# Merging two evictions, moving scale steps on VectorE, and moving the end of an attention chain by a third of an iteration

## The reference, cut to what matters

```python
x:  4 batches x 2048 tokens x 256
xn = layernorm(x)
# attention without softmax: per batch a 256 x 256 matrix and a bias
Q = l2norm(xn @ Wq.T + bq); K = l2norm(xn @ Wk.T + bk); V = xn @ Wv.T + bv
tailor = 1 / (L + Q . (sum(K) + EPS))
s = xn + gamma * (sum(V) + Q^T (K V)) * tailor
# feed forward, every operand quantized and dequantized to FP4 in blocks of 16
gate, up = fp4(xn) @ fp4(w_gate).T, fp4(xn) @ fp4(w_up).T        # 256 -> 704
g = silu(fp4(silu(gate) * up) @ fp4(w_down).T)                   # 704 -> 256
out = x + s * g
```

## Time and profile before

| | |
|---|---|
| median of three runs | 593.37 us |
| the profiled execution | 593.2 us, of which 591.5 us are the span from first to last instruction |
| PE busy | 547.5 us (93%) |
| DVE busy | 554.6 us (94%) |
| ACT, POOL busy | 415.6 us (70%), 243.4 us (41%) |
| granted TensorE clock | 0.987 over the span |

### The profile page before, as it was taken

The page is one execution under the profiler, slowest core; times in us unless marked ns, Lnnn a source line. Parts: engine busy times, 40 slices in busy tenths (PEclk is TensorE's granted clock), DMA queues, the critical chain, the costliest instruction groups (busy, mean ns, idle before and its releaser), DMA issues. The chain is left out here.

```text
span 591.5 us, 15211 instructions
## 1 busy us (share of the span) xinstructions
PE 547.5 (93%) x4973; PEld 424.9 (72%) x4973; DVE 554.6 (94%) x1180; ACT 415.6 (70%) x902; POOL 243.4 (41%) x213
## 2 busy tenths in 40 slices
PE   0478999999999999999999989999999999999996
PEld 0356777778787777778787767778787777778875
DVE  6998999999999999999999997999999999987783
ACT  4979888877787787767676766777776777555431
POOL 6524433333434434434443343444343344422146
PEclk9969899999999999999999999999999999999999
DMA  8010000000011001111011111110111101103124
GB/s 253 18 37 19 19 20 19 19 20 19 19 37 37 19 2 57 55 55 55 33 44 36 54 58 56 55 36 27 49 54 55 56 37 38 37 33 129 37 95 174
DMA packets 17633, 29.15 MB, mean 49 GB/s; under 512 B 2704, under 2 KB 5136, under 8 KB 17552
## 3 DMA queue, kind: packets, MB, share of 16 engines
q1 hardware_dynamic: 17552, 28.13, 14.3%
HBM read 19.73 MB, written 8.39 MB: 48 GB/s over the span
## 5 line engine op out<-in xcount | busy, mean ns | idle before, releaser
L1495 PE MATMUL GU<-wgu,xqT 128*128 128x352 f16 x1536 | 253.7, 316 | 3.6 <-issue 2.3
L1495 PEld LDWEIGHTS GU<-wgu,xqT 128*128 128x128 f16 x1536 | 148.5, 99 | 78.2 <-issue 3.4
L564 POOL TENSOR_TENSOR ht<-h,hrr 128x1408 f32<-128x1408 f32 x32 | 82.9, 2589 | 80.2 <-DVE hrr L992 78.7
L659 ACT ACTIVATE sil<-GU,wkap 128x352 f32<-128x352 f32 x128 | 70.7, 552 | 55.7 <-PE GU L1495 54.8
L1505 PE MATMUL DS<-wdT,hqT 128*128 128x256 f16 x704 | 87.3, 272 | 0.6 <-ACT hqT L666 0.6
L523 POOL TENSOR_TENSOR xnat<-xs,xnat 128x510 f16<-128x510 f32 (+1 forms) x32 | 37.0, 1157 | 106.1 <-DVE hq L1026 89.7
L1026 DVE TENSOR_TENSOR hq<-hg,hs 128x704 f16<-128x704 f16 x128 | 79.1, 658 | 1.0
L978 DVE SCALAR_TENSOR_TENSOR h<-GU,wkap,sil 128x352 f32<-128x352 f32 x128 | 68.7, 537 | 11.6 <-ACT sil L659 8.0
L1505 PEld LDWEIGHTS DS<-wdT,hqT 128*128 128x128 f16 x704 | 66.8, 98 | 10.4 <-ACT hqT L666 0.9
L513 POOL TENSOR_TENSOR rs<-ve,half 128x2 f32<-128x2 f32 x32 | 23.8, 744 | 110.0 <-DVE ht L1015 106.1
L695 ACT ACTIVATE gring<-DS,hun 128x256 f32<-128x256 f32 (+1 forms) x64 | 29.8, 465 | 42.9 <-issue 29.1
(11 more groups left out here) (176 smaller groups left out, 954.9 us busy)
## 6 DMA issues: line engine op xcount, KB each, us to landing
xin<-in_L_attn_x SPq DMA_DIRECT2D x34, 256.0 KB, 2.8
xe<-in_L_attn_x SPq DMA_DIRECT2D x24, 256.0 KB, 2.8
out<-o SPq DMA_DIRECT2D x24, 256.0 KB, 2.0
algebra<-in_L_ffn_w_down SPq DMA_DIRECT2D x1, 704.0 KB, 7.3
gring<-in_L_ffn_w_up SPq DMA_DIRECT2D x1, 640.0 KB, 6.1
xs<-in_L_attn_x SPq DMA_DIRECT2D x2, 256.0 KB, 4.2
xt<-in_L_attn_x SPq DMA_DIRECT2D x2, 256.0 KB, 4.8
out<-xin SPq DMA_DIRECT2D x2, 256.0 KB, 2.0
```

Source lines behind the costliest of these rows:

```text
L564: g.tensor_tensor(paired(ht[:, 0:2 * I]), paired(h[:, q]), spread(hrr[:, q], 4 * CB), ALU.mult).then_inc(S["ht_d"], 1)
L659: a.activation(sil[:, c], GU[:, c, 0, 0:CH], ACT.Silu, scale=wkap[:, 0:1]).then_inc(S["sil_d"], 1)
L1495: last = t.matmul(GU[:, c, m, 0:CH], xqT[:, k, j, 2 * a_ + kc], wgu[:, b_, kc, 2 * m + c], start=(z == 0 and kc == 0), stop=(z == 2 and kc ...
```

## The change

Three things change. The two y pieces of j = 0 are made by one instruction (`e_row`), which stands where the second one stood and counts two, except at `FIRST`. On DVE `x_scales` 1, 3 and 2 and `parts` 2 now stand ahead of `x_round` 0 and 1, and the y piece (1,0) stands behind `h_round` 2. In the attention tables the steps "top" and "high_low" are asked and answered elsewhere: "top" moves from (4,1,2) to (5,0,0) on PE and (5,0,1) on DVE, "high_low" from (5,0,1) to (5,0,2) on PE and from (5,0,4) to (5,0,2) on DVE. No tile, buffer or transfer changes.

```diff
-                (2, 1, 2): "norms", (3, 0, 2): "raw", (3, 1, 2): "tailor", (4, 0, 2): "product", (4, 1, 2): "top",
-                (5, 0, 1): "high_low"}
+                (2, 1, 2): "norms", (3, 0, 2): "raw", (3, 1, 2): "tailor", (4, 0, 2): "product", (5, 0, 0): "top",
+                (5, 0, 2): "high_low"}
...
-                   (3, 0, 0): "norms", (4, 0, 0): "tailor", (4, 0, 3): "scale", (4, 1, 0): "product", (4, 1, 2): "top", (5, 0, 4): "high_low"}
+                   (3, 0, 0): "norms", (4, 0, 0): "tailor", (4, 0, 3): "scale", (4, 1, 0): "product", (5, 0, 1): "top", (5, 0, 2): "high_low"}
...
+            def e_row(p, k, j):
+                e, q, row = s_place(p, k, j)
+                halves = lambda ap: ap.rearrange("p (c n) -> p c n", c=2)
+                wait(dve, "s_d", 4 * e + 2 * row + 2)
+                wait(dve, "g_d", 2 * e + row + 1)
+                v.scalar_tensor_tensor(halves(y[:, q, row * D:(row + 1) * D]), GU[:, :, 1, CH:CH + P], unm[:, 0:1],
+                                       halves(ring(gring, e, GRING)[:, row]), ALU.mult, ALU.mult).then_inc(S["y_d"], 2)
...
-                if s_beside(p, 0, tail):
-                    e_half(p, k, 0, 0, last_halves(0, i))
                 if s_beside(p, 0, tail) and last_halves(0, i):
+                    e_half(p, k, 0, 0, True)
                     e_half(p, k, 0, 1, True)
...
                 if s_beside(p, 0, tail) and not last_halves(0, i):
-                    e_half(p, k, 0, 1)
+                    e_row(p, k, 0)
...
                 attention(0, 2)
-                if on["xb"]:
-                    x_round(p, k, 0)
-                    x_round(p, k, 1)
-                if on["mb"]:
-                    parts(p, k, 2)
                 if on["xa"]:
                     x_scales(p, k, 1)
                 if on["xb"]:
                     x_scales(p - 1, 1 - k, 3)
+                if on["xa"]:
+                    x_scales(p, k, 2)
+                if on["mb"]:
+                    parts(p, k, 2)
+                if on["xb"]:
+                    x_round(p, k, 0)
+                    x_round(p, k, 1)
                 attention(0, 3)
                 if on["mb"]:
                     h_round(p, k, 0)
-                if on["xa"]:
-                    x_scales(p, k, 2)
                 if on["m"]:
                     h_mul(p, k, 1, 0, i)
-                if s_beside(p, 1, tail):
-                    e_half(p, k, 1, 0)
                 if on["xb"]:
                     x_round(p, k, 2)
...
                 if on["mb"]:
                     h_round(p, k, 2)
+                if s_beside(p, 1, tail):
+                    e_half(p, k, 1, 0)
                 if on["m"]:
                     h_mul(p, k, 1, 1, i)
```

## The result

The changed kernel takes 596.16 us (median of 7 runs, 594.67 to 597.98); the kernel before, on the same chip, takes 593.01 (7 runs, 592.32 to 593.45). The ratio is 1.0057, with a 95% interval of 1.0046 to 1.0068: 3.2 us slower, with 596.0 forecast. The profiled execution took 596.73 us, of which 595.0 are the span; it is 3.5 above the one of before. PEclk was 0.991.

A forecast was written before the change was run, and what follows sets the result against it. DVE was taken to set the pace, with PE having under 5 us of slack per batch. Terms +1.5 (first eleven iterations), -0.25 (iteration 11), +0.8 (loop), +0.8 (end) total +2.85 on 593.2: 596.0 us, range 589 to 599.

The forecast's parts named there:

- Merge: One 128x256 y instruction on DVE instead of two y pieces saves 0.13 us in each of 19 iterations.
- Dependent neighbours: DVE scale steps that read the result just ahead (xss behind xam, xrr) cost 0.14 us more in 29 iterations.
- Rival D: DVE steps reading the result just ahead cost nothing extra, so 4.1 us go away: 591.9 us; chance 0.03.
- Port waits at xt: With scale steps standing beside POOL's o instead of xt, DVE saves 1.9 us per batch; new loss 1.35.
- Port waits at hq: With y (1,0) between, the second hq pair meets POOL's xnat 0.26 us later, saving 2.1 per loop batch.
- Stalls of the lead: gate_up waits for later y, so DVE stalls at i = -1 and 0, 1, 2, 4: 3.9 us per batch.
- high_low: Now behind PE's down product, this attention step comes later than DVE wants it: 0.3 us stall in i = 5.
- The loop's +0.4 per batch: Eight loop iterations: DVE's own work changes by -3.8 us, new stalls add +4.2, so +0.4, twice.
- Iteration 11: Change of -0.25 us in this iteration: +0.14 for scale steps, -0.13 for merged y, -0.26 at hq.
- The end: From iteration 28 PE's chain runs to the end; gate_up (0,0) of 30 comes at 523.3, not 522.14: +0.8 us.
- Rival C: gate_up (1,0) waits for h (0,1); 20 iterations each pay about 0.25 us, loop lumps in full: 601; chance 0.07.
- Rival B: Gains and losses cancel: DVE gives up port waits where it then waits for PE; 593.3 us; chance 0.15.

## Why the prediction was right, and where only its sum was

The mechanism was right in part. DVE does save work and gets waits for PE in its place, whose gate_up is told of its free bank too late; y (1,0) late on the kernel before, and early in the changed one, show it from both sides. But the forecast had the loss in the wrong place. By its terms the late y costs -4.2 - 0.3 + 7.8 + 0.8 = +4.1 and the scale order 29 x 0.14 - 3.8 = +0.3. Each alone measured +1.2 and +3.1. That 596.0 stands beside 596.2 is luck in good part: terms missed in opposite ways.

- *Merge, -0.13 in 19 iterations.* Mis-sized: alone it gives -0.8 in all for -2.5, and nothing in the loop's batches, where -0.9 each was forecast, since there POOL's o sets when xt may begin.
- *Dependent neighbours, +0.14.* Right, a little small: +0.15 to +0.18 in iterations 1 to 7; nothing in 8 and 9, where silu already held h (1,0). The hole behind xam is in the rows (345.40 + 0.68 to 346.11). What was missed: h (1,0) now stands behind ht rather than behind xrr, and its start to start goes from 0.40 to 0.49. Rival D falls.
- *Port waits at xt, -1.9 per batch.* The step that failed. "xam, xss, xs, xrr stand where xt stood" treated xss as free beside POOL, as ham, h and y had been read to be. It is not, as the scale order with o whole and with o cut show. Alone, that order makes the batches 0.56 and 0.70 longer; less 8 x 0.16 for the dependence, 0.6 to 0.7 of the 1.9 is left. What the forecast named did come: xt takes 0.68 throughout, and hs is stretched in i = 3, to 1.30. What it left out is xss, which loses 1.8 and 1.0 us in the two batches of the changed kernel.
- *Port waits at hq, -2.1 per batch.* Right: 1.34 for 1.61, -0.26 per iteration with y late alone.
- *Stalls of the lead, +3.9 per batch.* Right in kind and place, too large in size: 0.44 and 0.76 in i = 1 (1.0 forecast), 1.19 + 0.39 in i = 2 (1.1 + 0.8), at most 0.40 at i = 0 (0.5), none at i = 4 (0.5). With "high_low", 0.38 and 0.35 for 0.3, that is 2.4 and 3.1 per batch for 4.2. Here the forecast was 1.1 to 1.8 too high per batch, and at xt and the merge together some 2.2 too low. The loop's +0.4 per batch came out as +0.5 to +0.6 because these errors went against each other; the terms as measured alone do not sum to it exactly.
- *Iteration 11, -0.25.* Failed: +1.18. y (1,0) early in iteration 10 alone brings -0.22, and the rows put the difference down to the clock. The forecast walked PE's work at one speed only and did not ask what a new stand-still does to PE's own rate.
- *The end, +0.8.* +1.6; gate_up (0,0) of iteration 30 started at 527.03. Without the 2.85 us of shift at the last ham of the loop (494.96 for the 492.11 of before), that is 524.2 for 523.3. With y (1,0) late alone iterations 29 and 30 grew by 1.9, so it is the lead again; which of the waits in them I had walked too short is not settled.
- *Rival C* did not come: in the loop there is no wait in every iteration. *Rival B* described the first eleven iterations and the loop well, and failed by iteration 11 and the end, +2.8 of the +4.9.

What stays open: the parts alone sum to 0.8 more than the whole, which is within the intervals of four ratios; which waits at the end were walked too short; and what decides whether the clock falls behind a stand-still of 2 us.

## What to carry to other kernels

Taking a wait off the busiest engine pays only if the next instruction is not held by the same thing: look at what will stand in its place, and put there reductions or reads of PSUM, not another SBUF-to-SBUF operation, however small. An instruction that frees a buffer for another engine should go as early as it can, even at the price of one more instruction, if the other engine has little lead left. Here merging them cost 3.3 us in the kernel with ham moved, and gained 0.8 in the slower kernel before. Where a move makes TensorE stand still in one more place, look at the granted clock behind it before the sum is believed.

## What the runs showed of the hardware

- A 128x32 TENSOR_SCALAR from one SBUF tensor to another is held by a GpSimd add that reads SBUF: 0.65 to 0.77 us beside it in iteration 19, 0.18 with the add gone. The 128x512 and 128x1408 reductions keep their 0.68 and 1.61 in such a place.
- TensorE ran at the lower of its levels, 1.2 GHz, for some 3.4 us after it had stood for 2.09 us (changed kernel) and 2.65 us (y late alone). It did so at the loop's back edge after 2.00 us too, but not after 2.05 us (changed kernel with y early), not after 2.31 us (kernel before) and not after 1.65 us. Taking away the first of these stand-stills, and the slow stretch with it, gave 1.1 us of kernel time (596.16 to 595.09).
- On VectorE the same 128x352 instruction h took 0.48 us and cost 0.40 behind the 128x88 and 128x32 reciprocals, where it waited for nothing, and took 0.57 to 0.58 and cost 0.49 to 0.50 behind a 128x1408 instruction, behind hq and behind y. It is not the size of the one ahead: behind the 128x2 reciprocal it took 0.56 to 0.58.
